# One stage for per-head attention and the finish, with V projected transposed

## Chip, cores, metric

One core of one Trainium2 chip. The metric is the device time of one launch in microseconds (us), median of three runs.

## The reference

Two transformer layers with adaptive layer norm on x of shape (4, 512, 512), all float32. The change touches the second layer's attention and what follows it:

```
q = (x @ Wq.T + bq).reshape(B, S, H=32, D=16)        # k, v alike
scores = einsum('bshd,bsgd->bshg', q, k) / sqrt(D)   # heads against heads, for each token
scores = where(scores > 0.001, scores, -inf)
out = einsum('bshg,bsgd->bshd', softmax(scores), v).reshape(B, S, 512) @ Wo.T + bo
x = x + ga * out
h = layernorm(x) * (1 + cb) + sb
logits = h @ route_w.T                               # 8 experts, the best one
x = x + gb * (w_best * (h @ A[e].T) @ Bw[e].T)       # LoRA experts of rank 16
```

Attention is between the 32 heads of one token: for each token a 32x32 matrix of scores over 16 dimensions. ga, gb, cb, sb come from a modulation computed once.

## The kernel before

The four sequences are worked in two halves of two batches (`HB = 2`, `nc.Fori(0, B // HB)`), 1024 tokens each. A half is a row of stages. A stage (class `Stage`, line 59) holds its own buffers and semaphores and ends with a barrier of all engines; within it each engine has a program of its own in written order, and semaphores order them. The residual stream `x` lies in SBUF as eight tiles of 128 tokens, four a batch.

The stages of the second layer:

- `stage_norm` (L338), layer norm with the features transposed and split into a high and a low part (`hh`, `hl`). ScalarE's queue first loads the QKV weights (`ahead.load`, L472), then ScalarE casts their high parts (`his`, L473), then scales the transposed features (L478).
- `stage_qkv` (L1082), 24 items of (weight, batch, 128 rows), 12 matmul passes each. k and q are projected with the dimensions on the partitions (dimension d of head h at row 32 d + h), ScalarE adds the bias (L1146), VectorE transposes 32x32 blocks (L1157), SyncE stores to the DRAM tensors `kp`, `qp` (L1112), one DMA an item. V is projected with the tokens on the partitions, VectorE adds the bias (L1160), SyncE stores to `vp` (L1109), one DMA an item.
- `stage_head_attention` (L1181), called heads in the trace. Eight units (`u`) of 128 tokens, two chunks (`c`) a unit, 16 chunks. SyncE loads for a unit: `qq` (one DMA, 64 partitions), `kd`, a block-diagonal K (four DMAs of 16 partitions with 4 KB in one piece each), and `bd`, a block-diagonal V with a column of ones (four DMAs of 32 partitions, pieces of 16 floats). Three buffers of each (`NU = 3`). A chunk: PE writes scores for 64 tokens (L1276), ScalarE copies them out (L1314), VectorE takes the maximum (L1327), GpSimd subtracts it (L1377), ScalarE exponentiates (L1305), VectorE applies the threshold (L1332) and transposes (L1339), PE weighs V (L1290, four chunks later, `LAG = 4`), VectorE divides by the ones column's sum (L1346, L1348). Scores and weighing run as four groups of 32 array columns. After unit 2 SyncE also loads gates, the output bias, `Wo` and the LoRA weights (L1259). GpSimd adds the gated output bias to `x` in the last ten chunks (L1388). At the end the outputs `o` are gathered to `at` by 32 DMAs of 64 KB (L1227), 24 on SyncE's queue and 8 on ScalarE's.
- `stage_finish` (L1392), called fin: projections (L1459), residual and statistics (L1550 to L1554), the Newton steps for the reciprocal root (L1568 to L1571), normalised tiles (L1573), transposes (L1469), scaled features (L1513), down projections with the router's columns (L1477), choice of the expert (L1581 to L1590), transposed weights (L1486, L1523), up projections (L1494), gating (L1600), the last add on GpSimd (L1451), and the store (L1444).

SBUF sets the ring sizes. `NR` is the ring of `sc`, `prob`, `pt` and `top`, `NS` the banks of scores, `NO` the banks of weighed outputs.

## Time and profile before

| | us |
|---|---|
| median of 3 runs | 2438.26 (2437.78 to 2439.22) |
| the profiled execution's own time | 2441.18 |
| its span, first to last instruction | 2439.5 |
| attention stage, first half | about 1095.7 to 1180 |
| finishing stage, first half | about 1180 to 1248 |
| the same two, second half | about 2283 to the end |

Busy shares of the span: PE 83%, VectorE (DVE) 62%, GpSimd (POOL) 45%, ScalarE (ACT) 41%. 155,621 DMA packets, 74,916 of them under 512 bytes. Times in the rows are us from the span's start, those of single instructions ns. An arrow in brackets names what ended the idle time before an instruction. PEclk is TensorE's granted clock as a share of 2.4 GHz. SPq is SyncE's DMA queue; its row gives the time of issue, not of transfer.

### The profile page before, as it was taken

The numbers are of one execution on the slowest core, as the hardware profiler recorded it, in microseconds if no ns is written. First come the engines' busy times: TensorE is split into PE (matmuls) and PEld (weight loads), VectorE is DVE, ScalarE is ACT, GpSimd is POOL, SyncE is SP. The second block draws the span as 40 slices with busy tenths as digits, with TensorE's granted clock in tenths as the row PEclk, the third lists the DMA queues.
The fourth block names the chain that finished last, engine by engine and source line by source line (L and its number), as shares of the span: only waits on it lengthen the run. The fifth ranks groups of instructions, "written<-read, shape, count | busy, mean of one in ns | idle before, by whom it ended". The sixth has DMA issues, their size and how long they took to land. (4 is left out here: it accounts for less than half of the span.)

```text
span 2439.5 us, 34037 instructions
## 1 busy us (share of the span) xinstructions
PE 2028.1 (83%) x11760; PEld 1647.2 (68%) x11760; DVE 1521.8 (62%) x3719; ACT 1010.6 (41%) x2344; POOL 1088.2 (45%) x848
## 2 busy tenths in 40 slices
PE   7389999999999983386747999999999999438667
PEld 1378888888888863274426888888888888326544
DVE  1666666666666668725655666666666666793355
ACT  1255555555555541212124555555555555212211
POOL 0455545545545443605026554545555455342331
PEclk9699999999999996695778999999999999768758
DMA  5300001000010010239230001001000010012760
GB/s 238 113 18 27 18 27 44 18 27 25 30 34 18 27 40 9 69 94 147 38 122 27 20 30 38 18 27 44 18 27 18 27 44 18 22 65 62 134 96 35
DMA packets 155621, 119.09 MB, mean 49 GB/s; under 512 B 74916, under 2 KB 118948, under 8 KB 154420
## 3 DMA queue, kind: packets, MB, share of 16 engines
q1 hardware_dynamic: 142228, 99.19, 15.6%
q10 hardware_dynamic: 13216, 17.65, 2.3%
q8 instruction: 97, 1.59, 0.3%
q14 instruction: 80, 0.66, 0.1%
HBM read 95.81 MB, written 16.81 MB: 46 GB/s over the span
## 5 line engine op out<-in xcount | busy, mean ns | idle before, releaser
L993 POOL TENSOR_TENSOR gqa_rot<-gqa_rot,consts 128x512 f32<-128x512 f32 x160 | 209.3, 1308 | 641.0 <-ACT gqa_rot L814 640.8
L830 ACT ACTIVATE gqa_prob<-gqa_prob,gqa_nmax 128x128 f32<-128x128 f32 (+3 forms) x512 | 282.5, 554 | 199.3 <-DVE gqa_nmax L915 199.3
L915 DVE CUSTOM_DVE_ANT_0 gqa_prob<-gqa_pS,consts 128x128 f32<-128x128 f32 (+3 forms) x512 | 220.3, 486 | 74.1 <-PE gqa_pS L714 73.1
L923 DVE TENSOR_TENSOR gqa_ptl<-gqa_pT,gqa_pth 128x384 fp32r<-128x384 f32 (+1 forms) x384 | 218.3, 597 | 31.4 <-ACT gqa_pth L840 26.9
L840 ACT CAST gqa_pth<-gqa_pT 128x384 fp32r<-128x384 f32 (+1 forms) x384 | 182.8, 511 | 94.2 <-PE gqa_pT L729 94.1
L996 POOL TENSOR_TENSOR gqa_full<-gqa_full,gqa_rot 128x512 f32<-128x512 f32 x160 | 206.9, 1293 | 12.6
L768 PE MATMUL gqa_pW<-woh,gqa_oh 128*128 128x512 f32 x504 | 202.6, 402 | 9.0 <-DVE y L940 9.0
L458 PE MATMUL ln_pT<-consts,ln_xn 128*128 128x128 f32 x192 | 45.2, 422 | 196.7 <-DVE ln_xn L437 196.7
L687 PE MATMUL gqa_pj<-first_hh,wqh 128*128 128x512 f32 x496 | 205.4, 414 | 0.0
L768 PE MATMUL gqa_pW<-woh,gqa_ol 128*128 128x512 f32 x504 | 197.2, 391 | 0.0
L1005 POOL TENSOR_TENSOR gqa_ql<-gqa_full,gqa_qh 128x512 fp32r<-128x512 f32 x128 | 164.6, 1286 | 73.1 <-DVE gqa_qh L904 73.1
L768 PE MATMUL gqa_pW<-wol,gqa_oh 128*128 128x512 f32 x504 | 196.4, 390 | 0.0
L687 PE MATMUL gqa_pj<-first_hh,wql 128*128 128x512 f32 x496 | 194.5, 392 | 0.0
L687 PE MATMUL gqa_pj<-first_hl,wqh 128*128 128x512 f32 x496 | 193.8, 391 | 0.0
L712 PE MATMUL gqa_pS<-gqa_kh,gqa_qh 128*128 128x192 f32 (+3 forms) x512 | 173.0, 338 | 19.2 <-POOL gqa_ql L1005 18.4
L729 PE MATMUL gqa_pT<-consts,gqa_prob 128*128 128x128 f32 x1280 | 182.9, 274 | 2.1 <-DVE gqa_ptl L923 2.1
L932 DVE TENSOR_SCALAR gqa_prob<-gqa_prob,gqa_rden 128x128 f32<-128x128 f32 (+3 forms) x512 | 178.0, 411 | 4.6
L729 PEld LDWEIGHTS gqa_pT<-consts,gqa_prob 128*128 128x128 f32 x1280 | 156.0, 141 | 36.1 <-DVE gqa_ptl L923 3.0
L750 PE MATMUL gqa_pO<-gqa_pth,gqa_vh 128*128 128x512 f32 (+3 forms) x512 | 166.9, 326 | 14.2 <-DVE gqa_ptl L923 14.2
L940 DVE TENSOR_TENSOR y<-gqa_pW,y 128x512 f32<-128x512 f32 x252 | 171.9, 682 | 8.1 <-PE gqa_pW L768 5.6
L458 PEld LDWEIGHTS ln_pT<-consts,ln_xn 128*128 128x128 f32 x192 | 38.3, 223 | 204.0 <-DVE ln_xn L437 204.0
L873 ACT CAST gqa_oh<-gqa_pO 128x512 fp32r<-128x512 f32 x128 | 75.3, 588 | 238.4 <-PE gqa_pO L750 238.4
(208 smaller groups left out, 5110.8 us busy)
## 6 DMA issues: line engine op xcount, KB each, us to landing
raw_q<-in_wq SPq DMA_DIRECT2D x16, 1024.0 KB, 5.4
raw_o<-in_wo SPq DMA_DIRECT2D x16, 1024.0 KB, 5.2
mod_wm<-in_wmod SPq DMA_DIRECT2D x8, 1536.0 KB, 19.8
raw_kv<-in_wkv SPq DMA_DIRECT2D x16, 512.0 KB, 6.7
x<-in_x SPq DMA_DIRECT2D x4, 1024.0 KB, 6.4
kp<-qkv_rest SPq DMA_DIRECT2D x16, 256.0 KB, 2.3
qp<-qkv_rest SPq DMA_DIRECT2D x16, 256.0 KB, 2.3
vp<-qkv_rest SPq DMA_DIRECT2D x16, 256.0 KB, 2.3
```

Of the source, the lines that this page charges most:

```text
L687: mm = pe.matmul(bank[e][:], wp, hp[:, k, t], start=(n == 0), stop=(n == 3 * KT - 1))
L712: pe.matmul(out, qh[r][:, t], kh[u % 2][:, 0:wide], start=True, stop=False)
L729: mm = pe.transpose(pT[k % 2][:, c:c + P], prob[n % 2][:, P_OFF[i] + j * P:P_OFF[i] + (j + 1) * P], held.ident)
L768: mm = pe.matmul(wbank(d)[:], op[h % 4][:, t], wp[:, h % R0, :], start=(m == 0), stop=(m == 5))
L830: ins = nc.scalar.activation(p, p, ACT.Exp, scale=-1.0, bias=nmax[r][:, i:i + 1], accum_out=den[r][:, i:i + 1])
L840: nc.scalar.copy(pth[:, c:c + w], pT[k % 2][:, 0:w]).then_inc(pt_hi, 1)
L915: nc.vector.tensor_tensor_reduce(prob[r][:, P_OFF[i]:P_OFF[i] + w], pS[s][:, c:c + w], held.mask[:, T - w:T], -1.0, LARGEST, ALU.add, ALU.min,
L923: nc.vector.tensor_tensor(ptl[:, c:c + w], pT[k % 2][:, 0:w], pth[:, c:c + w].bitcast(F32), ALU.subtract).then_inc(pt_lo, 1)
L932: ins = nc.vector.tensor_scalar(p, p, rden[n % 2][:, i:i + 1], None, ALU.mult)
L940: nc.vector.tensor_tensor(y[:, j, :], wbank(d)[:], y[:, j, :], ALU.add).then_inc(w_added, 1)
L993: nc.gpsimd.tensor_tensor(rot[r % 2][:], rot[r % 2][:], held.sinT, ALU.mult).then_inc(sined, 1)
L996: nc.gpsimd.tensor_tensor(full[r % 2][:], full[r % 2][:], rot[r % 2][:], ALU.add).then_inc(roped, 1)
```

## The change

1. `stage_head_attention` and `stage_finish` become one stage, `stage_heads_and_finish` (called tail), with the order of every engine written out. Batch 0's projections stand between the last weighings; batch 1's gathers wait for batch 0's projections (`at` now holds one batch); batch 1's projections stand between the ups of batch 0. Projections, transposes, downs and ups share three PSUM banks (`pG`) in the order of the list `users`.
2. Two units of q and k share one buffer, on partitions 0 to 63 and 64 to 127, so four units are in flight (`NK = 4`) with one `kd` to be zeroed instead of two. V keeps three buffers (`NV`). `NR` goes from 5 to 4, `NS` from 4 to 2, `NO` from 4 to 3.
3. V is projected like q and k, with dimensions on the partitions. ScalarE adds the bias and writes the tokens permuted, SyncE stores with four DMAs an item to `vp` of shape (batch, residue, head, dimension, token). `bd` has the token as its innermost index: a load moves pieces of 32 tokens (128 bytes), and a weighing matmul's moving operand has a step of 32 floats from column to column.
4. Gates, `Wo` and LoRA weights are loaded on ScalarE's queue in the norm stage before (between `ahead.load` and `ahead.his`); the output bias is gated and added on GpSimd in `stage_qkv`.

```diff
@@ stage_norm
+                for loaded in later:
+                    loaded.landed(sp)
...
                 if ahead:
                     ahead.load(act)
+                    for loaded in later:
+                        loaded.load(act)
                     ahead.his(act)
@@ stage_qkv: SyncE, ScalarE, GpSimd
+                        for d in range(4):
+                            sp.dma_start(a["vp"][b, :, :, 4 * m + d].rearrange("r g x -> g r x"),
+                                         src[32 * d:32 * d + 32].rearrange("p (r x) -> p r x", r=4)).then_inc(stored[n % NB], 16)
...
+                        nc.scalar.activation(rest[n % NB][:].rearrange("p (r l j) -> p j r l", r=4, j=4),
+                                             ps[n % 8][:].rearrange("p (j r l) -> p j r l", j=4, r=4), ACT.Identity,
+                                             bias=bias[:, w, m:m + 1]).then_inc(v_left, 1)
...
-                        nc.vector.tensor_tensor(rest[n % NB][:], ps[n % 8][:], vbias[:], ALU.add).then_inc(turned, 1)
...
+                for j in range(NT):
+                    pool.wait_ge(bias_gated, j // TT + 1)
+                    nc.gpsimd.tensor_tensor(held.x[:, j, :], held.x[:, j, :], bg[:, j // TT], ALU.add).then_inc(biased, 1)
@@ stage_heads_and_finish
-        NR, NS, NO, NU = 5, 4, 4, 3
-        bd = [st.sb(f"bd{i}", [P, 4, 4 * LU, VW]) for i in range(NU)]
+        NR, NS, NO, NK, NV = 4, 2, 3, 4, 3
+        bd = [st.sb(f"bd{i}", [P, 4, VW, 4 * LU]) for i in range(NV)]
+        at = st.sb("at", [P, KT, T])
...
-                src = a["vp"][b, t0:t0 + KT * LU, :].rearrange("t (g x) -> g t x", g=H1)
-                eng.dma_start(bd[u % NU][32 * r:32 * r + 32, r, :, 0:D1], src).then_inc(v_in[u], 16)
+                eng.dma_start(bd[u % NV][32 * r:32 * r + 32, r, 0:D1], a["vp"][b, r, :, :, 4 * l0:4 * l0 + 4 * LU]).then_inc(v_in[u], 16)
...
-                                         bd[u % NU][:, :, s0 + 4 * l + j, :], start=True, stop=True)
+                                         bd[u % NV][:, :, :, s0 + 4 * l + j], start=True, stop=True)
...
+                # SyncE, after the unit loads
+                sp.wait_ge(o_left, HALF)
+                for j in range(TT):
+                    gather(sp, 0, j)
+                sp.wait_ge(o_left, CHUNKS)
+                sp.wait_ge(p_full, TT)
+                for j in (0, 2):
+                    gather(sp, 1, j)
...
+                # PE
                 for c in range(CHUNKS + LAG):
                     if c < CHUNKS:
                         scores(c)
                     if c >= LAG:
                         weigh(c - LAG)
+                    if c >= FIRST_O:
+                        project(c - FIRST_O)
+                turns_and_downs(0)
+                project(4)
+                turn_weights(0)
+                project(5)
+                up(0)
+                project(6)
+                up(1)
+                project(7)
+                up(2)
+                up(3)
+                turns_and_downs(4)
+                turn_weights(1)
+                for j in range(TT, NT):
+                    up(j)
...
+                # ScalarE, in place of blocks of four tiles
+                def features_and_lowered(j):
+                    feature(j)
+                    feature(j + 1)
+                    feature(j + 2)
+                    lowered(j)
+                    feature(j + 3)
+                    lowered(j + 1)
+                    lowered(j + 2)
+                    lowered(j + 3)
...
+                # VectorE
+                for c in range(CHUNKS + BEHIND):
+                    if c >= BEHIND:
+                        output(c - BEHIND)
+                    if c < CHUNKS:
+                        tops(c)
+                    if 2 <= c < CHUNKS + 2:
+                        threshold(c - 2)
+                        transpose(c - 2)
+                    if FIRST_R <= c < FIRST_R + TT:
+                        residual(c - FIRST_R)
+                normalise(0)
+                choose(0)
+                residual(4)
+                residual(5)
+                gated(0)
+                residual(6)
+                gated(1)
+                residual(7)
+                normalise(1)
+                gated(2)
+                gated(3)
+                choose(1)
```

The lines that begin with # in the diff say which engine's program follows. `LAG` is 4, `BEHIND` 6, `FIRST_O` is `CHUNKS` = 16, `FIRST_R` is 18. PE's order within `turns_and_downs(j)` is turn j, j+1, j+2, down j, turn j+3, down j+1, j+2, j+3.

## Rows read from the trace of the kernel before

**Rows 1.** Busy by stage: us, then PE, PEld, DVE, ACT, POOL, PEclk, DMA share, GB/s.
```profile
1095.70:1180.00 84.30, 46.89 (x1024) 36.49 (x1024) 46.27 (x85) 21.86 (x33) 42.47 (x37) 0.50 0.89 136
1180.00:1248.00 68.00, 53.62 (x184) 30.19 (x184) 35.70 (x104) 8.82 (x18) 9.98 (x8) 0.90 0.08 31
```
**Rows 2.** PE in order of time: start, us, instruction, [idle before <- releaser].
```profile
1101.18 3.64 PE L1276 MATMUL heads_pS<-y,heads_qq 64*32 64x128 f32 x64 [9.56 <-DMA y<-kp]
...
1111.04 1.93 PE L1276 MATMUL heads_pS<-heads_kd,heads_qq 64*32 64x128 f32 x32 [2.81 <-DMA heads_kd<-kp]
1112.89 1.13 PE L1290 MATMUL heads_pO<-heads_bd,heads_pt 128*32 128x68 f32 x32
1113.96 1.93 PE L1276 MATMUL heads_pS<-heads_kd,heads_qq 64*32 64x128 f32 x32
...
1135.62 1.93 PE L1276 MATMUL heads_pS<-heads_kd,heads_qq 64*32 64x128 f32 x32 [11.80 <-DMA heads_kd<-kp]
...
1159.08 1.93 PE L1276 MATMUL heads_pS<-heads_kd,heads_qq 64*32 64x128 f32 x32
...
1180.19 29.09 PE L1459 MATMUL fin_ps<-out_w,at 128*128 128x512 f32 x64 [9.70 <-PEq L81]
```
**Rows 3.** SyncE's queue in order of time: start, us of issue.
```profile
1135.30 0.72 SPq L1216 DMA_DIRECT2D heads_qq<-qp  x1
1136.06 1.97 SPq L1220 DMA_DIRECT2D heads_kd<-kp  x4
1138.08 4.28 SPq L1237 DMA_DIRECT2D heads_bd<-vp  x4
...
1160.03 17.17 SPq L1227 DMA_DIRECT2D at<-heads_o  x24
```
**Rows 4.** DMA issues of the attention stage: count, KB each, median us to landing.
```profile
at<-heads_o SPq DMA_DIRECT2D x24, 64.0 KB, 2.2
heads_kd<-kp SPq DMA_DIRECT2D x20, 64.0 KB, 3.7
```
**Rows 5.** VectorE in order of time, the first half's finish.
```profile
1185.29 0.69 DVE L1550 TENSOR_TENSOR fin_yg<-fin_ps,out_ga 128x512 f32<-128x512 f32 x1 [13.23 <-PE fin_ps L1459]
...
1197.65 0.36 DVE L1561 BATCH_NORM_AGGREGATE fin_mv<-fin_stats 128x2 f32<-128x6 f32 x4
...
1201.04 1.91 DVE L1573 TENSOR_SCALAR fin_xn<-x,fin_mv,fin_rstd 128x512 f32<-128x512 f32 x4
```
**Rows 6.** Groups by line and shape, 1095 to 1260: count, busy us, mean ns.
```profile
L1290 PE MATMUL heads_pO<-heads_bd,heads_pt 128*32 128x68 f32 x512 | 17.9, 321 | 4.1 <-DVE heads_o L1348 4.1
L1276 PE MATMUL heads_pS<-y,heads_qq 64*32 64x128 f32 x192 | 11.4, 417 | 11.4 <-DMA y<-kp 11.4
L1348 DVE TENSOR_TENSOR heads_o<-heads_pO,heads_rden 128x256 f32<-128x256 f32 x16 | 9.7, 607 | 0.5
L1550 DVE TENSOR_TENSOR fin_yg<-fin_ps,out_ga 128x512 f32<-128x512 f32 x8 | 5.5, 687 | 17.3 <-PE fin_ps L1459 17.3
L1346 DVE RECIPROCAL heads_rden<-heads_pO 128x16 f32<-128x16 f32 x16 | 3.6, 222 | 0.0
```
**Rows 7.** The finish in order of time: PE's transposes, routing, and the last ups.
```profile
1209.12 1.91 PE L1469 MATMUL fin_pT<-consts,fin_xn 128*128 128x128 f32 x16
...
1219.78 0.19 DVE L1581 TENSOR_REDUCE fin_top<-fin_hs 128x4 f32<-128x32 f32 x1 [3.09 <-ACT fin_hs L1519]
...
1237.51 5.40 PE L1494 MATMUL fin_ps<-lora_wB,fin_wtT 128*128 128x512 f32 x8 [0.67 <-ACT fin_wtT L1523]
```
**Rows 8.** QKV stage: VectorE's V add.
```profile
1091.72 0.69 DVE L1160 TENSOR_TENSOR qkv_rest<-qkv_ps,qkv_vbias 128x512 f32<-128x512 f32 x1 [2.11 <-PE qkv_ps L1130]
```
**Rows 9.** ScalarE in the norm stage before QKV: casts of weights, then features.
```profile
988.95 2.18 ACT L258 CAST qkv_wh<-qkv_raw 128x512 fp32r<-128x512 f32 x4 [45.32 <-DMA qkv_raw<-in_w1k]
991.60 2.18 ACT L258 CAST qkv_wh<-qkv_raw 128x512 fp32r<-128x512 f32 x4 [0.47 <-DMA qkv_raw<-in_w1q]
...
1001.23 2.79 ACT L478 ACTIVATE ln_hf<-ln_pT,modh 128x512 f32<-128x512 f32 x4 [4.81 <-PE ln_pT L458]
```

More of the change, by code:

```diff
@@ L246, in load @@
     def load(self, act):
[L247 to L249 removed]
+        for i in range(3):
+            act.dma_start(self.bias[:, i], self.a[("b1q", "b1k", "b1v")[i]]).then_inc(self.b_came, 16)
         for i in QKV_ORDER:
@@ L335, in load_gates, with stage_norm @@
     eng.wait_ge(sem, 16 * HB)
-def stage_norm(nc, held, a, layer, which, half, residual=None, weights=None, ahead=None):
+def stage_norm(nc, held, a, layer, which, half, residual=None, weights=None, ahead=None, later=()):
     with Stage(nc, f"ln{layer}{which}") as st:
@@ L472, in _ @@
                     ahead.load(act)
+                    for loaded in later:
+                        loaded.load(act)
                     ahead.his(act)
@@ L1178, with stage_heads_and_finish @@
 CHUNKS = UNITS1 * CU
-def stage_head_attention(nc, held, a, ahead, ob, kd0, at):
-    with Stage(nc, "heads") as st:
-        NR, NS, NO, NU = 5, 4, 4, 3
-        qq = [st.sb(f"qq{i}", [P, LU, P]) for i in range(NU)]
-        kd = [kd0] + [st.sb(f"kd{i}", [P, 4, 4 * LU, H1]) for i in range(1, NU)]
-        bd = [st.sb(f"bd{i}", [P, 4, 4 * LU, VW]) for i in range(NU)]
+LAG = 4
+BEHIND = 6
+FIRST_O = CHUNKS
+FIRST_R = CHUNKS + 2
+def stage_heads_and_finish(nc, held, a, kd0, out, ws, gates, half):
+    with Stage(nc, "tail") as st:
+        NR, NS, NO, NK, NV = 4, 2, 3, 4, 3
+        x, ga, gb, NA = held.x, gates.ga, gates.gb, ws.NA
+        kd = [kd0, st.sb("kd1", [P, 4, 4 * LU, H1])]
+        qq = [st.sb(f"qq{i}", [P, LU, P]) for i in range(NK // 2)]
+        bd = [st.sb(f"bd{i}", [P, 4, VW, 4 * LU]) for i in range(NV)]
         sc = [st.sb(f"sc{i}", [P, TC, H1]) for i in range(NR)]
@@ L1239, in stage_head_attention, with gather @@
+        def gather(eng, b, j):
+            for q in range(4):
+                src = o[b][32 * j:32 * j + 32].rearrange("p (k q) r l -> p q k (r l)", q=4)[:, q]
+                eng.dma_start(at[32 * q:32 * q + 32, :, j * P:(j + 1) * P], src).then_inc(at_in[b][j], 16)
         with nc.Block() as block:
@@ new lines, in turn, with down @@
+                def turn(j):
+                    pe.wait_ge(xn_done, j + 1)
+                    wait_bank(pe, "t", j)
+                    for k in range(KT):
+                        mm = pe.transpose(bank("t", j)[:, k * P:(k + 1) * P], xn[:, j % TT, k * P:(k + 1) * P], held.ident)
+                    mm.then_inc(x_turned, 1)
+                def down(j):
+                    pe.wait_ge(scaled, KT * (j + 1))
+                    wait_bank(pe, "a", j)
+                    for k in range(KT):
+                        mm = pe.matmul(bank("a", j)[:, 0:NA], hf[:, j % TT, k], ws.wA[:, k, :],
+                                       start=(k == 0), stop=(k == KT - 1))
+                    mm.then_inc(a_full, 1)
@@ new lines, in turn_weights, with up @@
+                def turn_weights(b):
+                    pe.wait_ge(routed, b + 1)
+                    wait_bank(pe, "w", b)
+                    for j in range(TT):
+                        mm = pe.transpose(bank("w", b)[:, j * P:(j + 1) * P], wt[:, j, :], held.ident)
+                    mm.then_inc(w_turned, 1)
+                def up(j):
+                    pe.wait_ge(w_left, j // TT + 1)
+                    wait_bank(pe, "u", j)
+                    pe.matmul(bank("u", j)[:], wtT[:, j % TT * P:(j % TT + 1) * P], ws.wB[:], start=True, stop=True).then_inc(z_full, 1)
@@ L1528, in _ @@
+                act.wait_ge(p_full, TT)
+                for j in (1, 3):
+                    gather(act, 1, j)
+                features_and_lowered(0)
                 weights_left(0)
-                lowered(1)
+                features_and_lowered(4)
                 weights_left(1)
@@ L1605, in _, with gated @@
-                for b in range(HB):
-                    choose(b)
-                    finish(b)
+                def gated(j):
+                    dve.wait_ge(z_full, j + 1)
+                    if j >= 2:
+                        dve.wait_ge(added, j - 1)
+                    nc.vector.tensor_tensor(zg[j % 2][:], bank("u", j)[:], gb[:, j // TT], ALU.mult).then_inc(z_gated, 1)
+                nc.vector.memset(bd[0][:], 0.0).then_inc(v_zeroed[0], 1)
+                dve.wait_ge(v_zeroed[0], 1)
@@ new lines, in _ @@
+                for r in range(4):
+                    nc.vector.memset(bd[0][32 * r:32 * r + 32, r, D1], 1.0).then_inc(ones[0], 1)
+                for c in range(CHUNKS + BEHIND):
[8 more added lines that the diff above has]
+                        residual(c - FIRST_R)
```

514 lines of the change are left out of this document (211 added, 303 removed), and 4 rows, old and new, of the table users.

## The prediction

> **What bounds the kernel now.** The diff leaves the first layer alone, so I read the second layer's last two stages, which run twice (once a half); the times below are of the first half. First the table by stage: the attention stage takes 84.3 us and the finishing stage 68.0 us, and in neither is any compute engine near full; in the attention stage the DMA engines are, at 0.89 of the stretch [rows 1]. Then TensorE's order of time. A chunk inside a loaded unit takes 2.93 us: scores at 1111.04, weighing at 1112.89, the next scores at 1113.96. Between units PE waits for `kp`, 11.8 us of it at 1135.62 [rows 2]. SyncE's queue says why. One unit issues one DMA of q, four of k (1.97 us) and four of values (4.28 us). q and k go at half a microsecond a DMA, the values at 1.07, although k's and v's DMAs move 64 KB each: the values come as 1024 pieces of 64 bytes, the k's as 16 pieces of 4 KB. Units follow each other at 7.1 us (1135.30 to 1142.36), against 5.86 us of compute. After unit 2 the queue also issues 2.5 MB (by their shapes) of gates, biases and weights ahead of the k that PE then waits for: the 11.8 us hole [rows 3, 4]. After the last output the gather, a barrier and the first projection pass, 13.2 us, before VectorE works again at 1185.29 [rows 5]. So: transfers bound the attention stage, a chain of short dependent steps the finishing one.
>
> **The change, part by part** (first half; then doubled).
>
> (a) Attention up to its last scores. Weights and gates move into the norm stage before, behind the six DMAs of ScalarE's queue. The hole goes if that stage hides them: they stand behind the QKV weights in the same queue, ScalarE is idle for 45 us before its cast at 988.95 and again for 4.8 us before 1001.23, so the 2.5 MB (6.6 us at the rate at which the 1 MB weights let ScalarE's casts begin, 2.65 us apart) and eight issues (0.5 us each, 4 us) fit [rows 9]. Without that cover up to 4 us would come back; I take 0. Values come in 512 pieces of 128 bytes. Not in the trace; bounds a DMA: 0.49 us (the k's, 16 pieces) to 1.07 us (no gain from fewer pieces). I take half of 1.07, 0.55 to 0.6, so issue is 0.5 + 2.0 + 2.3 = 4.8 us a unit, less than the compute's 5.86. Two units of q/k share one buffer by halves of the partitions, four in flight instead of three, so none waits late. Start: scores of unit 0 begin as before (1101.18). Queue: q,k(0) 2.5, q,k(1) 2.5, v(0) 2.3, q,k(2) 2.5 from 1095.7 gives 1105.5, plus 3.7 landing is 1109.2: chunk 4. Eleven more chunks at 2.93 put chunk 15's scores at 1141.5 instead of 1159.08: **-17.5 us** [rows 2 to 4]. Rings shrink (scores 4 to 2 banks, outputs 4 to 3, SBUF rings 5 to 4): PE's next but one scores need only ScalarE's 0.59 us copy, and weighing c-4 needs output c-7, a step earlier on VectorE. Cost 0, at worst 0.3 us a chunk.
>
> (b) Weighing with the token innermost: the moving operand of 68 columns now steps 128 bytes at each column instead of 4. No row shows such a matmul. What rows say: passes of 128 and 68 columns last 417 and 321 ns, 1.6 ns a column, though they start 58 and 33 ns apart: four column groups run side by side, each taking an element every 1.6 ns. VectorE's strided write of the output (128x256) takes 607 ns where a line through 128x16 (222 ns) and 128x512 (687 ns) gives 447: 1.56 ns an element against 0.94. A strided element thus costs just about what a stream already allows [rows 6]. Bounds: 0 (a wider step can't make the same reads quicker), and full loss of the side-by-side streams, 68 x 1.6 = 109 ns a pass, 32 passes 3.5 us instead of 1.07: +2.4 us a chunk. I take +0.1, a tenth of 1.07, by the nearest row: **+1.6 us** over 16 chunks.
> The Trainium skill (SBUF - State Buffer, under "Door 1: The DMA port swizzle") says that SBUF is read in lines of 16 bytes and that two hits on a line are wanted for full rate. VectorE's row above agrees in kind (1.7 times an element). By it TensorE's strided pass would take about twice as long, and the sum would be rival 1's, 2432. No run here shows that for a matmul yet.
>
> (c) Drain and batch 0's projections. Before: from chunk 15's scores (1159.08) to the first normalised tile of batch 0 (1201.04), 42.0 us [rows 2, 5]. After: v(7) is issued at about 1141, then sixteen gathers at 0.72 us (17.17/24): tile 0 lands at 1146.1, the next every 2.9 us [rows 3, 4]. PE takes weigh 11, 12, then project(0) at 1146.1, 5.1 us as the first one now (1180.19 to 1185.29), weigh 13, project(1) 3.43 us (29.09 less 5.1, over seven), weigh 14, project(2), weigh 15, project(3): 1164.7. Residual 2.1 us and the Newton chain 3.4 us (1197.65 to 1201.04) give 1170.2: 28.7 us, **-13.4 us** [rows 2, 5].
>
> (d) The rest. One buffer `at` serves both batches and PE's order puts batch 0's transposes first, so batch 1's projections no longer hide beneath normalise(0). From 1170.2: first tile 0.5; transposes, features and down in tile order, now 10.7 us for four (1209.12 to 1219.78), I estimate 9.5 since one 2.8 us feature block is no longer waited for whole; project(4) to (7) at 3.4, a weight transpose 0.7, two ups 0.9 between: 1196.4; residual 2.1, normalise 3.4, tile 0.5, 9.5, route 2.5, its way back 1.3, ups 5.9 (the last four begin at 1237.51, their last gating at 1243.4), and 4.5 from there to the end of the stretch, 1248, the last add and store: 1226.1. That is 55.9 us against 46.9 (1201.04 to 1248): **+9.0 us** [rows 1, 5, 7].
>
> (e) QKV stage. V's projection keeps its 12 passes a tile and its 2.8 us pace; a 0.69 us ScalarE activation (strided write; to 1.2 us) replaces VectorE's 0.69 us add. Each tile issues four stores instead of one (4 x 0.5 = 2.0 us, less than 2.8), of 512-byte pieces as k and q have. Only the last tile shows: three more issues, **+1.6 us** [rows 3, 8]. The bias work (ten adds of 1.3 us) goes to GpSimd in this stage, where it has nothing behind its memset: 0.
>
> Sum: -17.5 + 1.6 - 13.4 + 9.0 + 1.6 = -18.7 us a half, -37.4 in all. From the profiled execution's own 2441.18 (span 2439.5) that is 2403.8; the median lies 2.9 below that execution, so 2401.
>
> **Rivals.**
> 1. The strided moving read has no slack and pays VectorE's factor, 1.7, rounded up to 2 on a whole pass (1.07 to 2.14 us a chunk, +17 us a half instead of +1.6): -3.3 a half, about 2432. For: VectorE's 1.7 times; against: a stream's slack of 1.6 ns.
> 2. The other side: the four column groups cannot read strided side by side. Place: L1290's matmuls; price 2.4 us a chunk, 39 us a half, less 20.3: +18.5 a half, 2475. It decides for slower once a pass costs over 73 ns (1.07 + 20.3/16 = 2.3 us a chunk over 32 passes). For: 128 bytes is 32 times the element; against: VectorE's row loses 1.7 times, not three.
> 3. 128-byte pieces cost twice a 64-byte one: v stays at 1.07 us a DMA, units at 7.1 us, 1.2 us over the compute for the six after the start; only the hole goes. +8 us a half: 2417. For: nothing shows 128 bytes; against: k's DMAs.
> 4. The written order costs: project(0..3) wait for gathers behind v(7), hold weigh 13 to 15, and run at the half clock that the attention stage shows (0.50, [rows 1]), 7 us each instead of 3.4 to 5.1: +7 to 9 a half, 2418.
>
> **Numbers.** Forecast with small misses 0.55, 2401 (own range 2388 to 2412); rival 1 0.15; rival 2 0.10; rival 3 0.08; rival 4 0.12. Range 2385 (0 for (b), a cheaper (d) by 6 us a half) to 2440 (rival 1 with small misses). A measurement here tells about 0.2% (5 us) from no change. Faster: 0.55 + 0.12 + 0.08 + most of rival 1, less something for what no rival names: 0.80. Same 0.05, slower 0.15.
>
> **What would show it.** Passes of L1290's successor about 33 to 37 ns apart (rival 1: 67, rival 2: 109); scores of chunk 4 near 13.5 us and of chunk 15 near 46 us after the stage starts; no PE wait for `kp` over 1 us; value DMAs issued 0.5 to 0.6 us apart; first normalised tile of batch 0 near 75 us; stage end near 130 us where the two now take 152; nothing longer in the norm stage. The prediction is wrong if chunks follow each other slower than 3.2 us, or if PE stands still over 8 us between project(3) and the first transpose.

## The result, and the profile after

| | before | after |
|---|---|---|
| median of the runs side by side | 2438.74 us (2437.78 to 2441.68) | 2400.81 us (2397.88 to 2404.07) |
| ratio | | 0.984, 95% interval 0.9825 to 0.9861 |
| span of the profiled execution | 2439.5 | 2396.9 |
| layer 2's last part, first half | 158.1 (1095.70 to 1253.77) | 140.8 (1094.46 to 1235.29) |
| the same, second half | 156.3 (2283.17 to the end) | 134.9 (2262.02 to the end) |

The forecast was 2401: the kernel is faster, by the amount foreseen. Of the 42.6 us between the two spans, 38.7 come from the merged stage (17.2 and 21.5) and 3.9 from the norm and QKV stages ahead of it, which the forecast had 3.2 us longer.

The page first: fewer small packets, and a busier PE at a higher clock.

```profile
PE 2025.7 (85%) x11760; PEld 1648.7 (69%) x11760; DVE 1501.5 (63%) x3703; ACT 1039.6 (43%) x2408; POOL 1085.8 (45%) x846
DMA packets 129765, 118.57 MB, mean 49 GB/s; under 512 B 43172, under 2 KB 95396, under 8 KB 128564
```

The table by stretch of the kernel after (columns as in [rows 1]: stretch, length, busy time and count of PE, weight loads, VectorE, ScalarE, GpSimd, then PEclk, DMA share, GB/s). Two columns answer to [rows 1]: the DMA share is 0.63 to 0.72 (0.69 from the stage's start to 1145) where it was 0.89, and the clock, 0.50 all through the stage before, reaches 1.00 after 1110.

```profile
1110.00:1122.00 12.00, 10.74 (x252) 8.18 (x244) 9.13 (x17) 4.62 (x8) 5.57 (x4) 0.88 0.72 125
1122.00:1145.00 23.00, 19.53 (x488) 15.23 (x492) 18.83 (x36) 8.12 (x15) 10.03 (x8) 1.00 0.63 120
```

TensorE in order of time answers to [rows 2]. The first line is chunk 4. Scores start 1.86 us apart from the weighing behind them at 1109.50 and 1.01 us from 1112.93 on; the weighing takes 1.57 us (1111.36 to 1112.93) where it took 1.07. The hole of 11.8 us is gone; waits for `kp` of 0.2 to 2.8 us are left. Chunk 15 is at 1143.73. Projections and weighings then alternate, and PE stands still for 6.10 us for the first normalised tile.

```profile
1109.50 1.93 PE L1333 MATMUL tail_pS<-tail_kd,tail_qq 64*32 64x128 f32 x32 [2.83 <-DMA tail_kd<-kp]
1111.36 1.65 PE L1347 MATMUL tail_pO<-tail_bd,tail_pt 128*32 128x68 f32 x32
1112.93 1.08 PE L1333 MATMUL tail_pS<-tail_kd,tail_qq 64*32 64x128 f32 x32
1113.94 1.63 PE L1347 MATMUL tail_pO<-tail_bd,tail_pt 128*32 128x68 f32 x32
...
1141.14 1.08 PE L1333 MATMUL tail_pS<-tail_kd,tail_qq 64*32 64x128 f32 x32 [2.36 <-DMA tail_kd<-kp]
1142.15 1.65 PE L1347 MATMUL tail_pO<-tail_bd,tail_pt 128*32 128x68 f32 x32
1143.73 1.08 PE L1333 MATMUL tail_pS<-tail_kd,tail_qq 64*32 64x128 f32 x32
...
1149.25 3.70 PE L1355 MATMUL tail_pG<-out_w,tail_at 128*128 128x512 f32 x8 [1.44 <-DMA tail_at<-tail_o]
...
1174.65 2.82 PE L1363 MATMUL tail_pG<-consts,tail_xn 128*128 128x128 f32 x12 [6.10 <-DVE tail_xn L1544]
```

SyncE's queue answers to [rows 3]. A value DMA takes 0.92 us here (3.69 for four; 2.56 to 3.84 over the stage, so 0.64 to 0.96 each) against 1.07 in [rows 3] (before's fours take 3.00 to 4.48 us over its stage, and 7.23 behind the weights), and a unit 6.4 us (1108.57 to 1114.98) against 7.1. The last line is the next half's first load.

```profile
1108.57 0.63 SPq L1276 DMA_DIRECT2D tail_qq<-qp  x1
1109.24 1.97 SPq L1281 DMA_DIRECT2D tail_kd<-kp  x4
1111.25 3.69 SPq L1290 DMA_DIRECT2D tail_bd<-vp  x4
1114.98 0.63 SPq L1276 DMA_DIRECT2D tail_qq<-qp  x1
...
1144.01 29.76 SPq L1296 DMA_DIRECT2D tail_at<-tail_o  x24
...
1235.29 1.26 SPq L370 DMA_DIRECT2D x<-in_x  x2
```

What nobody had forecast is in the norm stage. ScalarE, kernel after, against [rows 9] (there the casts began at 988.95 and the features at 1001.23):

```profile
983.09 1.32 ACTq L321 DMA_DIRECT2D out_ga<-gates  x2
...
986.58 2.88 ACTq L299 DMA_DIRECT2D lora_wA<-in_loraAT  x1
989.49 2.35 ACTq L300 DMA_DIRECT2D lora_wA<-in_routeT  x1
991.87 2.60 ACTq L301 DMA_DIRECT2D lora_wB<-in_loraBT  x1
994.57 6.34 ACT L257 CAST qkv_wh<-qkv_raw 128x512 fp32r<-128x512 f32 x12 [51.90 <-issue]
1000.82 2.76 ACT L481 ACTIVATE ln_hf<-ln_pT,modh 128x512 f32<-128x512 f32 x4
```

The eight added issues take 11.4 us (983.09 to 994.47), not 4: three of them 2.3 to 2.9 us each. The casts come 5.6 us later, and yet the features start 0.4 us earlier, and QKV's first bias 2.4 us earlier (1024.91 against 1027.31; 0.35 of it because the stage itself begins earlier). Experiment e5 below says why.

### The profile page after: what moved, and what is told of

Read it like the earlier page. It is cut to its first block and busy times, and to the rows that moved or that the text cites. A ratio compares the mean times of both kernels' runs of the same rounds, so it can differ in the third digit from the quotient of the medians.

```text
span 2396.9 us, 34177 instructions
## 1 busy us (share of the span) xinstructions
PE 2025.7 (85%) x11760; PEld 1648.7 (69%) x11760; DVE 1501.5 (63%) x3703; ACT 1039.6 (43%) x2408; POOL 1085.8 (45%) x846
## 3 DMA queue, kind: packets, MB, share of 16 engines
q8 instruction: 97, 1.59, 0.3%
```

## The experiments

Each ran with the kernel before beside it on the same chip. Between the sets (e1 to e4; e5 and e6; e7 to e10; e11 and e12) its median moved: 2440.6, 2441.8, 2442.0 and 2443.2 us, and 2438.7 beside the kernel after. So a time is compared with another set's by its ratio too (the kernel after: 0.9843).

**e1, the strided read taken away.** The weighing reads 68 neighbouring floats of the same buffer (weighed outputs are then not the reference's).

```diff
-bd[u % NV][:, :, :, s0 + 4 * l + j]
+bd[u % NV][:].rearrange("p j x s -> p (j x s)")[:, 68 * (s0 % 16 + 4 * l + j):68 * (s0 % 16 + 4 * l + j) + 68]
```

> The changed kernel, but each weighing matmul reads 68 neighbouring floats of the same V block instead of 68 floats 128 bytes apart (the values read are not the right ones; loads, counts and shapes stay). Theory 1 (the 128-byte step costs PE time: a pass starts every 49 ns in the changed kernel, where the old contiguous one started every 33 ns at half the clock): passes fall to 25 to 33 ns, a weighing from 1.57 to 0.8 to 1.1 us. Theory 2 (the step costs nothing, 49 ns has another cause): passes stay at 49 ns. On the clock: either it stays at 1.00 in the attention stage because the waits for k are gone (scores 1.0 us a chunk; the kernel then gains 0 to 4 us in all, VectorE's 2.65 us a chunk being next), or the long strided passes are what keeps it up and it falls back to 0.50 (scores 1.86 us, 2.93 us a chunk, the kernel 3 to 10 us slower).

Measured: 2396.57 us (2391.37 to 2399.95), ratio 0.982 (0.9806 to 0.9833). TensorE's order of time in e1: weighing 1.06 us in the stage (1110.56 to 1111.62, 33 ns a pass), scores back at 1.86, pace 2.93 us a chunk; in the drain, at full clock, one weighing lasts 0.61 us where the kernel after takes 1.57.

```profile
1110.56 1.13 PE L1347 MATMUL tail_pO<-tail_bd,tail_pt 128*32 128x68 f32 x32
1111.62 1.93 PE L1333 MATMUL tail_pS<-tail_kd,tail_qq 64*32 64x128 f32 x32
...
1151.66 0.68 PE L1347 MATMUL tail_pO<-tail_bd,tail_pt 128*32 128x68 f32 x32
```

And e1's table by stretch, to be read against that of after: the clock is 0.50 again, with PE busy 11.64 of 12 us.

```profile
1110.00:1122.00 12.00, 11.64 (x260) 8.85 (x256) 9.39 (x16) 4.48 (x8) 5.42 (x4) 0.50 0.73 132
1122.00:1145.00 23.00, 22.51 (x511) 17.25 (x507) 20.64 (x39) 8.96 (x16) 10.26 (x8) 0.50 0.63 122
```

What follows: the strided pass costs 49 ns against 33 at half clock and 19 at full, far more than the forecast's tenth. But with it the clock rises, and the scores pay back 0.85 us a chunk. Net, the stride costs 4 to 6 us in all (by the times 4.2, by the ratios 5.6; the ranges of the times still overlap, and e7 to e9 below find 5 us or more again). My expectation had the clock's fall right and its price wrong: it gave such a kernel 3 to 10 us more than after, and it takes 4 less.

**e2, the strided read alone**, put into the kernel before (again other outputs; V's layout is as before, so the elements read are not those of one token):

```diff
-bd[u % NU][:, :, s0 + 4 * l + j, :]
+bd[u % NU][:].rearrange("p j s x -> p (j s x)").rearrange("p (c s) -> p c s", s=4 * LU)[:, :, s0 + 4 * l + j]
```

> The kernel before, but each weighing matmul reads 68 floats 128 bytes apart (the values read are not the right ones; nothing else changes). Theory 1 (the step costs PE time): passes start 49 ns or more apart instead of 33, a weighing takes 1.6 to 2.1 us. Theory 2 (free): 33 ns. On the clock: if the strided passes raise PE's activity enough, the granted clock in the attention stage rises from 0.50 and the scores drop from 1.86 to 1.0 us; if the waits for k decide, it stays 0.50 and a chunk takes 3.5 to 4.0 us. Since transfers bound this stage at 7.1 us a unit, the time changes by -4 to +2 us in the first case and by 0 to +16 us in the second.

Measured: 2440.81 us (2435.26 to 2442.82), ratio 0.9996 (0.9987 to 1.0005). The same view shows the pass at 49 ns at either clock (1113.93 to 1115.51 is 1.58 us at the half clock, 1119.97 to 1121.56 is 1.59 at the full one), the scores falling from 1.86 to 1.01 us between, and the fall back behind the hole:

```profile
1113.93 1.65 PE L1290 MATMUL heads_pO<-heads_bd,heads_pt 128*32 128x68 f32 x32
1115.51 1.93 PE L1276 MATMUL heads_pS<-heads_kd,heads_qq 64*32 64x128 f32 x32
...
1118.96 1.08 PE L1276 MATMUL heads_pS<-y,heads_qq 64*32 64x128 f32 x32
1119.97 1.66 PE L1290 MATMUL heads_pO<-heads_bd,heads_pt 128*32 128x68 f32 x32
1121.56 1.08 PE L1276 MATMUL heads_pS<-y,heads_qq 64*32 64x128 f32 x32
...
1136.83 1.93 PE L1276 MATMUL heads_pS<-heads_kd,heads_qq 64*32 64x128 f32 x32 [12.61 <-DMA heads_kd<-kp]
```

So the read raises the clock by itself, and is worth nothing there: the transfers bounded that stage, as the forecast read it.

**e3, all but V's layout.** V projected, biased, stored, loaded and read as before; everything else (the merged order, four units in flight, the moved weights) as after. The main lines of the edit:

```diff
-eng.dma_start(bd[u % NV][32 * r:32 * r + 32, r, 0:D1], a["vp"][b, r, :, :, 4 * l0:4 * l0 + 4 * LU])
+src = a["vp"][b, t0:t0 + KT * LU, :].rearrange("t (g x) -> g t x", g=H1)
+eng.dma_start(bd[u % NV][32 * r:32 * r + 32, r, :, 0:D1], src)
...
-bd[u % NV][:, :, :, s0 + 4 * l + j]
+bd[u % NV][:, :, s0 + 4 * l + j, :]
```

> The changed kernel with V projected, stored, loaded (1024 pieces of 64 bytes a DMA) and read (contiguous) as in the kernel before: the merged stage alone. Theory 1 (the smaller number of pieces is worth 5 to 8 us a half, less 1 us in the QKV stage): 8 to 14 us slower than the changed kernel, value DMAs issued 1.07 us apart, units 7 us apart, clock back at 0.50. Theory 2 (what the loads gain, the strided read loses): within 3 us of the changed kernel.

Measured: 2403.79 us (2402.34 to 2405.91), ratio 0.9852 (0.9837 to 0.9867): 3 us slower than after, where my first theory had 8 to 14. SyncE's queue in e3:

```profile
1110.94 4.32 SPq L1296 DMA_DIRECT2D tail_bd<-vp  x4
1119.22 2.48 SPq L1296 DMA_DIRECT2D tail_bd<-vp  x4
```

Four value DMAs take 2.48 to 4.60 us, so 0.62 to 1.15 each: the shortest are as short as after's, the longest longer. Units come 6.9 us apart on the mean (1108.11 to 1135.53 for four) against 6.5 in after (1108.57 to 1134.48), and the queue reaches the first gather 53.7 us after the stage's start against 49.6. The clock is 0.50; chunk 15's scores come 52.7 us after the stage's start (after: 49.3). The stage starts 1.8 us earlier (1092.66 against 1094.46). Of that 1.2 us is the price of V's four stores an item and their strided activation: from QKV's first bias to the stage's start e3 and before take 68.4 us, after 69.6. The rest lies ahead of that bias. Nearly all of the gain, 36.8 of 37.9 us (each against the kernel before beside it), comes without V's new layout. How it divides between the merged order and the four units in flight no run shows; of the other parts only the weights have a run of their own, e4. By itself the 3 us between e3 and after is no more than the two ranges leave open; e10 below finds it again.

**e4, the weights loaded where they were**: `Wo` and the LoRA weights on SyncE's queue behind unit 3's q and k (the gates stay, the output bias needs them).

```diff
-ahead=qkv, later=(gates, out, lora)
+ahead=qkv, later=(gates,)
@@ SyncE, in the loop over units
+                    if u == NV:
+                        out.load(sp)
+                        ws.load(sp)
```

> The changed kernel with Wo and the LoRA weights (1.3 MB) loaded again on SyncE's queue after the third unit's values, not in the norm stage. Theory 1 (they stand ahead of a k load that PE waits for): a wait for kp of 4 to 7 us comes back, 8 to 14 us slower in all. Theory 2 (four units in flight and smaller value loads hide them): within 3 us. In the norm stage ScalarE's casts begin at about 8 us after its start instead of 14.6.

Measured: 2415.83 us (2413.08 to 2418.54), ratio 0.99 (0.9885 to 0.9916), 14 to 15 us slower than after. A wait for `kp` of 7.44 us is back in the first half, and the merged stage takes 144.9 us instead of 140.8. It also starts 2.7 us later (1097.12 against 1094.46): the norm stage is longer with only the gates' issues in front of its casts. By the profiles some 10 us of e4's loss lie in the merged stage (4.1 and 5.7 in the two halves) and 6 in the norm stage (2.9 and 3.3, from ScalarE's first issue to QKV's first bias).

```profile
1121.93 1.64 PE L1354 MATMUL tail_pO<-tail_bd,tail_pt 128*32 128x68 f32 x32
1131.01 1.93 PE L1340 MATMUL tail_pS<-y,tail_qq 64*32 64x128 f32 x32 [7.44 <-DMA y<-kp]
```

**e5, the norm stage.** The casts ahead of the eight issues:

```diff
+                    ahead.his(act)
                     for loaded in later:
                         loaded.load(act)
-                    ahead.his(act)
```

> The kernel after, with ScalarE casting the QKV weights' low parts' sources (the high parts) ahead of issuing the loads of gates, Wo and LoRA weights, as it did before the change. In the profile after, the eight extra issues hold ScalarE from 983.1 to 994.5, so its casts, and GpSimd's low parts behind them, begin some 5 us later than before; GpSimd then no longer works while VectorE does batch 0's Newton steps, and these take 0.16 us each instead of 1.13 to 1.20. Theory (VectorE's small operations suffer from GpSimd's tensor work beside them, and the delay of the casts removes that): the Newton steps of batch 0 are back at 1.1 to 1.2 us, QKV's first bias is 2 to 2.5 us later from the norm stage's start than in the kernel after, 4 to 5 us in all: about 2405. Rival (the norm stage got shorter for another reason, such as the barrier or buffers placed elsewhere): the Newton steps stay at 0.16 us and the time within 1.5 us of the kernel after, 2401. Second rival (the issues, now behind the casts, delay the scaled features by their 11 us of issue): the norm stage grows by 6 us or more a half, 2415.

Measured: 2407.02 us (2404.48 to 2407.93), ratio 0.9859 (0.9843 to 0.9874), and 47.7 us from ScalarE's first issue to QKV's first bias (979.42 to 1027.08) against 44.9 after (979.99 to 1024.91) and 47.0 before. In the second half it is 47.2 against 44.1 and 47.4. The same stretch in the first half is 43.7 to 46.3 in all ten profiles with the eight issues ahead of the casts and 47.0 to 47.8 in the four without (before, e2, e4, e5); in the second half 43.7 to 44.5 and 47.2 to 47.4. VectorE and GpSimd in e5; the Newton steps of batch 0:

```profile
988.99 0.17 DVE L429 TENSOR_SCALAR ln_var<-ln_mv 128x4 f32<-128x4 f32 x1
989.19 1.13 DVE L430 TENSOR_SCALAR ln_step<-ln_var 128x4 int32<-128x4 int32 x1
990.36 1.20 DVE L431 TENSOR_SCALAR ln_rstd<-ln_step 128x4 int32<-128x4 int32 x1
991.59 1.18 DVE L433 TENSOR_TENSOR ln_step<-ln_rstd 128x4 f32<-128x4 f32 x1
992.80 1.20 DVE L434 TENSOR_TENSOR ln_step<-ln_step,ln_var 128x4 f32<-128x4 f32 x1
994.03 0.17 DVE L435 TENSOR_SCALAR ln_step<-ln_step 128x4 f32<-128x4 f32 x1
```

```profile
989.03 4.95 POOL L260 TENSOR_TENSOR qkv_wl<-qkv_raw,qkv_wh 128x512 fp32r<-128x512 f32 x4
```

In the kernel after the same steps stand clear of GpSimd, which starts at 995.27:

```profile
989.75 0.17 DVE L430 TENSOR_SCALAR ln_step<-ln_var 128x4 int32<-128x4 int32 x1
989.95 0.17 DVE L431 TENSOR_SCALAR ln_rstd<-ln_step 128x4 int32<-128x4 int32 x1
990.15 0.16 DVE L433 TENSOR_TENSOR ln_step<-ln_rstd 128x4 f32<-128x4 f32 x1
```

```profile
995.27 6.68 POOL L260 TENSOR_TENSOR qkv_wl<-qkv_raw,qkv_wh 128x512 fp32r<-128x512 f32 x4 [5.65 <-ACT qkv_wh L257]
```

Four of GpSimd's operations, 1.24 us each, hold four of VectorE's, one each: 0.17 us of work becomes 1.2, and the first step behind 993.98, where GpSimd ends, is quick again. The kernel before has the same picture. What after gains by the delay (4.0 us in these four steps a half) it gives back in part: GpSimd's four then meet VectorE's additions and take 6.68 us, and three of batch 1's steps are held at 1.18 to 1.19 us in after as they are before. The Trainium skill (SBUF - State Buffer, "SBUF: two separate sides") says that VectorE, where its instruction has two inputs in SBUF or runs in a two-port mode, and GpSimd share a pair of ports, which one instruction holds to its end while the other waits. These rows agree: 1.13 to 1.20 us beside operations of 1.24.

**e6, a better place for batch 1's projections.** A second buffer for the gathered outputs (in the unused part of `y`), each projection of batch 0 one step later, and projections 4 and 5 in the two banks of scores, ahead of batch 0's transposes; VectorE's residuals move with them, and batch 1's gathers no longer wait for batch 0's projections. All of the work is done.

```diff
-        at = st.sb("at", [P, KT, T])
+        at = [st.sb("at", [P, KT, T]), held.y[:, 0:KT, :]]
...
+            if kind == "o" and j in (4, 5):
+                return pS[j - 4][:].rearrange("p t h -> p (t h)")
...
-                    if c >= FIRST_O:
-                        project(c - FIRST_O)
+                    if c >= FIRST_O + 1:
+                        project(c - FIRST_O - 1)
+                project(3)
+                project(4)
+                project(5)
                 turns_and_downs(0)
-                project(4)
+                project(6)
                 turn_weights(0)
-                project(5)
                 up(0)
-                project(6)
+                project(7)
                 up(1)
-                project(7)
                 up(2)
```

> The kernel after, all of the work done, with the gathered outputs in two buffers (the second in the free part of y), so that batch 1's gathers wait only for the last outputs; each of batch 0's projections one step later in PE's order; projections 4 and 5 in the two banks of scores, ahead of batch 0's transposes, where PE stands still for 6.1 us for the normalised tile. Theory (term (d), +8.5 us a half, is PE work that lost its place beneath normalise(0), together with the 6.1 us for which PE stands still): PE's stand before the first transpose is under 1 us, two projections of 3.6 us leave the stretch behind it, 6 to 7 us a half less: 2386 to 2390. Rival (the finishing part is a chain through VectorE and ScalarE, and PE's projections in it were hidden): the stand is only moved, the last normalise comes at the same distance, within 2 us a half: 2397 to 2401. Second rival (SyncE's gathers of batch 1 share the DMA engines with those of batch 0 and the later projections shift the residuals): 1 to 3 us a half more: 2404.

Measured: 2385.67 us (2384.96 to 2388.51), ratio 0.9772 (0.9759 to 0.9786): 15 us faster than after by the times, 17 by the ratios, 13 between the profiled spans. TensorE in e6: no stand ahead of the transposes at 1173.04, and the next half's load is at 1228.06, 133.9 us after the stage's start instead of 140.8 (second half 128.9 instead of 134.9). The parts of this edit were not run one by one.

```profile
1166.17 7.03 PE L1358 MATMUL tail_pS<-out_w,y 128*128 128x512 f32 x16
1173.04 1.47 PE L1366 MATMUL tail_pG<-consts,tail_xn 128*128 128x128 f32 x12
...
1197.81 1.11 PE L1366 MATMUL tail_pG<-consts,tail_xn 128*128 128x128 f32 x4 [4.99 <-DVE tail_xn L1547]
```

**e7 to e9, the step of the strided read.** As e1, with 68 elements 8, 16 or 64 bytes apart (S = 2, 4, 16; other outputs):

```diff
-bd[u % NV][:, :, :, s0 + 4 * l + j]
+bd[u % NV][:].rearrange("p j x s -> p (j x s)").rearrange("p (c s) -> p c s", s=S)[:, s0 % 16 + 4 * l + j:s0 % 16 + 4 * l + j + 68, 0]
```

> The kernel after, with the weighing matmuls reading 68 elements of V's buffer 8 bytes apart instead of 128 (so the weighed outputs are not the reference's; the number and shape of all instructions stay). A pass of 68 columns takes 49 ns at 128 bytes, and 33 ns (clock 0.50) or 19 ns (clock 1.00) with neighbours. Theory (reads come in lines of 16 bytes and want two hits on a line, as the Trainium skill's SBUF page has it for other readers): at 8 bytes there are two hits a line, so passes of 33 ns at half clock, no rise of the clock, time as with neighbours, 2396 to 2398. Rival (any gap at all costs the full price): 49 ns a pass and the clock at 1.00 in the attention stage, 2401.

> The same with a step of 16 bytes, one hit a line. Theory of 16-byte lines: the full price, 49 ns a pass, 1.57 us a chunk, clock 1.00: 2401. Rival (it is the size of the step, 32 columns of a larger unit, that costs): 33 ns at half clock, 2397.

> The same with a step of 64 bytes. Theory of 16-byte lines: as at 16 and 128 bytes, 49 ns a pass. Rival (conflicts between banks of SBUF, which depend on the power of two in the step): 64 bytes costs less than 128, between 33 and 49 ns, or the price falls by half from 128 to 64.

**e11 and e12, the step off the power of two.** e6 with one or four unused floats behind each row of 32 tokens, so 132 or 144 bytes; all of the work is done.

```diff
-        bd = [st.sb(f"bd{i}", [P, 4, VW, 4 * LU]) for i in range(NV)]
+        bd = [st.sb(f"bd{i}", [P, 4, VW, 4 * LU + 4]) for i in range(NV)]
...
-                eng.dma_start(bd[u % NV][32 * r:32 * r + 32, r, 0:D1], a["vp"][b, r, :, :, 4 * l0:4 * l0 + 4 * LU]).then_inc(v_in[u], 16)
+                eng.dma_start(bd[u % NV][32 * r:32 * r + 32, r, 0:D1, 0:4 * LU], a["vp"][b, r, :, :, 4 * l0:4 * l0 + 4 * LU]).then_inc(v_in[u], 16)
```

> The kernel with batch 1's first two projections ahead of batch 0's transposes (2385.67), all of the work done, with each row of 32 tokens in V's buffer followed by one unused float, so that the weighing's elements lie 132 bytes apart instead of 128. Pass times so far: 19 ns (neighbours, full clock), 21 (8 bytes), 35 (16 bytes), 36 (64 bytes), 49 (128 bytes). Theory (above 16 bytes the extra 14 ns of 128 bytes belong to the power of two: all elements of a column fall in the same part of the memory): a pass takes 35 to 36 ns, a weighing 1.1 us instead of 1.57, and the time is 1 to 3 us a half less: 2380 to 2384. Rival (the price grows with the distance alone): 49 ns or more, 2385 to 2386. Second rival (the loads write 128-byte pieces that no longer begin at a multiple of 16 bytes and become slower): value DMAs over 0.9 us apart throughout, 2388 to 2395.

> The same with four unused floats behind each row: elements 144 bytes apart, pieces that begin at multiples of 16 bytes. Theory of the power of two: 35 to 36 ns a pass, 2380 to 2384, and loads as they are. Rival of the distance: 49 ns or more, 2385 to 2386. If 132 bytes is quicker and 144 is not, what counts is where in a line of 16 bytes an element lies.

Measured, with the time from the start of a weighing to that of what follows it at full clock, over its 32 passes. PEclk is the mean of the stretch, between the two levels 0.50 and 1.00:

| step in bytes | one weighing, us | a pass, ns | PEclk 1110 to 1122 | time, us |
|---|---|---|---|---|
| 4 (e1) | 0.61 | 19 | 0.50 | 2396.57 |
| 8 (e7) | 0.66 | 21 | 0.50 | 2394.97 (2393.04 to 2396.02) |
| 16 (e8) | 1.11 | 35 | 0.93 | 2395.71 (2392.05 to 2398.47) |
| 64 (e9) | 1.15 | 36 | 0.91 | 2395.03 (2391.58 to 2395.38) |
| 128 (after) | 1.57 | 49 | 0.88 | 2400.81 |
| 128 (e6) | 1.57 | 49 | 0.90 | 2385.67 |
| 132 (e11) | 1.13 | 35 | 0.83 | 2385.88 (2383.91 to 2387.04) |
| 144 (e12) | 1.11 | 35 | 0.90 | 2384.81 (2383.87 to 2386.49) |

The rows behind three of them, e7, e8 and e12 in this order, each a weighing and its successor:

```profile
1153.43 0.72 PE L1347 MATMUL tail_pO<-tail_bd,tail_pt 128*32 128x68 f32 x32
1154.09 3.70 PE L1355 MATMUL tail_pG<-out_w,tail_at 128*128 128x512 f32 x8
```

```profile
1114.82 1.18 PE L1347 MATMUL tail_pO<-tail_bd,tail_pt 128*32 128x68 f32 x32
1115.93 1.08 PE L1333 MATMUL tail_pS<-tail_kd,tail_qq 64*32 64x128 f32 x32
```

```profile
1128.14 1.18 PE L1350 MATMUL tail_pO<-tail_bd,tail_pt 128*32 128x68 f32 x32
1129.25 1.08 PE L1336 MATMUL tail_pS<-y,tail_qq 64*32 64x128 f32 x32
```

What follows: there are two prices. One comes between 8 and 16 bytes (21 to 35 ns), the other, of the steps tried, at 128 bytes alone (49), and 132 and 144 bytes are free of it: "the price grows with the distance" is refuted, and so is my expectation for e8 and e9 that 16 bytes already has the full price. At the half clock the first price nearly vanishes: between scores of 1.86 us a weighing with 132 bytes takes 1.15 us (e11, 1130.88 to 1132.03), 36 ns a pass, where neighbours take 33. The clock rises with steps of 16 bytes and more, not at 4 and 8. With 128 bytes it then stays at 1.00 (after, 1122 to 1145), with 16 and 64 the mean of that stretch is 0.87 and 0.85. What raises it is open. PE is busy 8.72 of the 12 us in e8 and 11.64 in e1, but a higher clock shortens the busy time itself (scores 1.01 us instead of 1.86), so these two figures settle nothing.

What it is worth depends on what stands beside it. In the order of after, e8 ends the stage 136.8 us after its start (1093.11 to 1229.92) against 140.8, and in the second half takes 133.7 against 134.9; the times say the same, 2.5 us a half. One profile can't say where in the stage this lies: e8's chunk 15 has its scores at 48.2 us and after's at 49.3, but e6, whose attention part is that of after, has 48.2 too; and e5, whose whole stage is that of after, ends it at 139.2. e9, with e8's pass but its first projection partly at the half clock (5.3 us where the others take 3.63), ends at 139.6, and its time is e8's. In e6's order the same saving is lost: e12's first transpose is at 78.3 us after the stage's start against 78.9, its end at 133.6 against 133.9, and its time within 1 to 2 us of e6's. That part of my expectation (2380 to 2384) failed: units still arrive some 6.4 us apart and PE waits for `kp` instead (0.25, 1.91, 1.32, 2.03, 1.77 us in e12), and the weighing ahead of the first projection waits 1.46 us for VectorE's output.

**e10, e6 with V as before.** The same edits as e3.

> The kernel with batch 1's first two projections ahead of batch 0's transposes (2385.67), and V projected, stored, loaded and read as before the change; all of the work is done. In the kernel after, V the old way cost 3 us (2403.8 against 2400.8). Theory (the V layout saves about 2.2 us a half in the attention part and costs 1 us at QKV's end, apart from the rest): 2388 to 2390. Rival (the saving hangs on the full clock that the strided read brings, which the eager projections would make good themselves): no difference, 2385 to 2386.

Measured: 2390.49 us (2388.91 to 2392.94), ratio 0.9789 (0.9776 to 0.9803). V's layout is worth 4 to 5 us here (2390.49 less 2385.67; by the ratios 4.1), with ranges of the times that don't touch (by 0.4 us, and on another chip), so it pays, a little, independently of the projections' place. e6 and e12 are the fastest versions; between them no difference is shown.

## Why the prediction was right, and where it was not

In the main the mechanism held: the hole gone, the first projection pass beneath the last chunks, batch 1's projections out of their cover. Two parts of it did not: the transfers got cheaper by far less than I counted on, so that they still set the pace, and the strided read costs and gives back what no row had shown. By its steps, first half:

| step | forecast | measured |
|---|---|---|
| (a)+(b) to chunk 15's scores | -15.9 | -14.1 (63.4 to 49.3; second half -16.5) |
| (c) to the first normalised tile | -13.4 | -11.7 (42.0 to 30.3) |
| (d) from there to the end | +9.0 | +8.5 (52.7 to 61.2, each to the next half's first load) |
| (e) QKV's end | +1.6 | +1.2 (68.4 to 69.6 from QKV's first bias to the stage's start; second half the same) |
| norm stage | 0 | about -2.1 (second half -3.3) |

**(a)** Chunk 4 came at 15.0 us, not 13.5, and chunk 15 at 49.3, not 46 (with (b) 47.4; 47.2 in the second half). The mis-sized term is a value DMA: 0.64 to 0.96 us instead of 0.55 to 0.6. A unit takes 6.4 us to issue, not 4.8, so transfers still set the pace up to the last chunks, and the waits of 1.36 and 2.36 us break my "no wait over 1 us". From chunk 4 to 15 a chunk takes 3.11 us on the mean, waits included, close to the 3.2 that I had named as the sign of being wrong. e8 and e12 show this bound: 0.46 us less a chunk brings chunk 15 forward by nothing that the scatter lets one see (48.2 and 48.7 us, against 49.3 in after and 48.2 in e6). That V's layout buys something (against rival 3) is shown by e3 and e10, 2 to 5 us; but rival 3's price for the old pieces was far too high: e3, which has them, took 2404 and not 2417. The row that I halved, 1.07 us a value DMA, was no fixed price of 64-byte pieces: in e3 they take from 0.62 us up. That the moved weights end the hole is shown by e4; its 15 us hold 6 of the norm stage.

**(b)** The step's reasoning failed, its size in the end did little. I argued that a stream which takes an element every 1.6 ns has slack for a wide step. A pass went from 33 to 49 ns (rival 1 asked for 67, rival 2 for 109, the forecast for 33 to 37), so the side-by-side streams did lose half again. What I had no row for is that the clock rises with it, 0.50 to 1.00, and takes 0.85 us from the scores: a chunk without a wait takes 2.58 us, less than before (2.93). Net the stride costs 4 to 6 us by e1 and 5 to 10 by e7 to e9, in times and in ratios, where the forecast had 3.2. Part of it lies where I had not priced it, behind chunk 15's scores: there three weighings stand between projections at full clock, and each takes 1.57 us where neighbours take 0.61 (e1). The rule of the Trainium skill that the prediction quoted (SBUF - State Buffer, under "Door 1: The DMA port swizzle"), two hits on a line of 16 bytes, is borne out by e7 (8 bytes, 21 ns) and e8 (16 bytes, 35 ns): nearly the factor of two at full clock that the prediction worked out from it. At half clock neighbours already take 33 and the factor does not show. The 49 ns at 128 bytes are beyond this rule.

**(c)** Each projection is followed 5.2 us later by the next (3.63 plus a strided weighing of 1.57) instead of 4.5, and the first started 5.5 us behind chunk 15's scores instead of 4.6, its gather being issued at 1144.01 behind a late v(7). The stride is the term that was left out, 1.5 us; the later gather adds 0.9 and the passes of 3.63 instead of 3.43 add 0.6. The first projection, which I had at 5.1 us, took 3.63 and hid 1.5 of this. In e8 this stretch is 27.3 us (1141.27 to 1168.6, the start of the tile 0.6 us ahead of its transpose at 1169.21), below my 28.7. Rival 4 is refuted: the projections ran at full clock, 3.63 us. In e1, with neighbours read, project(0) did meet the half clock (5.6 us), which is rival 4's mechanism at a quarter of its price.

**(d)** Right in size; the 6.10 us for which PE stands still ahead of the transposes were in the forecast's sum without a name (I allowed up to 8). e6 shows that this stand and the projections behind it are one loss: with two of them put into it, 6.9 and 6.0 us come back in the two halves, most of (d).

**(e) and the norm stage.** (e) held, at 1.2 us. "Nothing longer in the norm stage" held, by luck: I took the eight issues for 4 us hidden beneath a wait. They take 11.4 and delay the casts; what made that harmless, and even a gain of 2 to 3 us a half, is the collision between GpSimd's low parts and VectorE's Newton steps that they move apart. e5 shows it: 4 us in all by the ratios, whose intervals still overlap, and 6 by the times and the spans; the profiles place these 6 in the norm stage (2.7 and 3.1 in the two halves).

**The sum.** For the profiled execution I had 2403.8, and it took 2398.6. The difference is -7.1 from what stands ahead of the merged stage (it starts 1.2 us earlier in the first half, and 2.7 more are gained before the second, where I had +1.6 each; 1.0 of these 3.9 us lies even ahead of the norm stages' first issue, and no part of the change explains it) and +1.9 from the merged stage (-17.2 and -21.5 against -20.3 each). I then took off 2.9 us because before's profiled execution lay above its median; after's lies 2.2 below its own. So the medians meet at 2401 by two misses of 5 us that cancel; the interval of the ratio (2396 to 2405 on 2438.7) holds both.

## What to carry to other kernels

Before judging a merge of stages by the work it overlaps, list what loses its cover: here a shared buffer forced half of the projections behind the point where TensorE stood idle, and a second buffer in unused space, with the order that it allows, gave back 13 to 17 us, about as much as the weights' new place with all that it set off (e4). Once transfers set the pace, a cheaper matmul turns into a wait (e12) and a dearer one is hidden (e2): take the price of a form of read from a row, but take its worth from the wait that stands next to it, stretch by stretch: the same quicker pass was worth about 2.5 us a half in one order and nothing that shows in another. Look at VectorE's chains of tiny operations beside GpSimd's long ones: a few instructions shifted on a third engine moved 4 to 6 us.

## What the runs showed of the hardware

- An fp32 matmul pass of 68 columns, in four column groups, started every 19 ns with neighbouring elements and 21 ns with a step of 8 bytes (clock 1.00), 35 to 36 ns with 16, 64, 132 or 144 bytes, and 49 ns with 128 bytes; the last at clock 0.50 and 1.00 alike. At 0.50 neighbours and 8 bytes took 33 ns and 132 bytes 36.
- The granted clock stayed at 0.50 through the attention part with neighbours or 8 bytes (before, e1, e3, e7, e10, both halves). With 16 bytes and more it rose behind the first weighings; means of 0.83 to 0.93 from 1110 to 1122. With 128 bytes it rose in the kernel before too (e2). What makes it rise is open.
- VectorE's operations on 128x4 took 0.16 to 0.17 us alone and 1.13 to 1.20 beside GpSimd's 128x512 subtraction of 1.24 us.
- Eight DMA issues on ScalarE's queue behind 3 MB of weights (by their shapes) took 11.4 us, three of them 2.3 to 2.9 each where the six ahead of them took 0.35 to 0.53, and ScalarE computed nothing meanwhile.
- A 64 KB load in 128-byte pieces took 0.64 to 0.96 us to issue (after), in 64-byte pieces 0.62 to 1.15 (e3); over all 32 loads of a stage the mean was 0.78 (after) and 0.74 (e6) against 0.84 (e3) and 0.94 (e10).
